# Seven experts' results turned by transposing DMAs of 16-bit planes and joined by VectorE, in place of TensorE's fp32 transposes

## What is computed

```python
for k in range(K):                       # K = 2 choices per token
    e = top_i[:, k]; w = top_p[:, k]
    ...                                  # place of the token in its expert's buffer, cap = 320
    buf = jnp.zeros((E, cap, D)).at[e, pos_c].set(xt * keep, mode='drop')
    h = gelu(jnp.einsum('ecd,edf->ecf', buf, w1) + b1[:, None, :])       # D = 512, f = 2048
    y = jnp.einsum('ecf,efd->ecd', h, w2) + b2[:, None, :]
    y = y + jnp.einsum('ecr,erd->ecd', gelu(jnp.einsum('ecd,edr->ecr', buf, wd)), wu)
    out = out + y[e, pos_c] * keep * w[:, None]
out = out + 0.2 * shared_expert(xt)
```

## Time and profile before

| | us |
|---|---|
| median of 3 executions | 1367.65 (1367.64 to 1367.82) |
| the profiled execution, its own time | 1367.89 |
| its span in the trace | 1366.1 |
| TensorE busy, share of the span | 96% |
| VectorE, ScalarE, GpSimd busy | 60%, 50%, 18% |
| mean granted clock of TensorE | 0.993 of full speed |

### The profile page before, as it was taken

One profiled execution on the slowest core, in us unless ns is written; L12 is line 12 of the kernel. 1 busy time (PEld: TensorE's weight loads), 2 busy tenths in 40 slices (PEclk: granted clock), 3 DMA queues, 4 the chain that ended last, 5 costly groups with the idle time before them and its releaser, 6 DMA issues.

```text
span 1366.1 us, 26996 instructions
## 1 busy us (share of the span) xinstructions
PE 1316.6 (96%) x11151; PEld 962.6 (70%) x11212; DVE 814.7 (60%) x1338; ACT 686.4 (50%) x1028; POOL 252.4 (18%) x219
## 2 busy tenths in 40 slices
PE   5788999999999999999999999999999999999997
PEld 2152736465564647384888889999999988888895
DVE  7786778697788887763643625536255363552620
ACT  4776666757576766662533524435244252442521
POOL 4730010000010050413200403003030040210202
PEclk9899999999999999999999999999999999999999
DMA  9613131413273232316635755457554675554403
GB/s 272 209 48 101 47 101 40 108 47 85 64 72 80 76 66 91 116 33 120 215 106 126 186 137 156 128 139 193 128 163 120 120 189 124 158 139 116 99 9 39
DMA packets 144939, 155.89 MB, mean 114 GB/s; under 512 B 67257, under 2 KB 87881, under 8 KB 144818
## 3 DMA queue, kind: packets, MB, share of 16 engines
q1 hardware_dynamic: 132530, 128.97, 34.8%
q0 software_dynamic: 12288, 25.21, 10.2%
HBM read 109.47 MB, written 34.15 MB: 105 GB/s over the span
## 4 chain that ended last, share of the span: by engine, by line
PE 82%; DVE 7%; ACT 6%; issue 4%; POOL 1%; DMA 0%; POOLq 0%; ACTq 0%; DVEq 0%
PE banks L1779 25%; PE banks L1809 24%; PE banks L1695 10%; PE banks L1713 9%; PE banks L1635 3%; PE banks L1583 3%; PE banks L1615 2%; DVE rowmax L1247 2%; ACT hidden L1036 2%; ACT QS L1023 2%; DVE late_stage L1268 1%; PE banks L1831 1%; PE banks L1644 1%; PE banks L1669 1%; ACT hf L1082 1%
## 5 line engine op out<-in xcount | busy, mean ns | idle before, releaser
L1809 PE MATMUL banks<-hidden,w2h 128*128 128x0 bf16 x2048 | 306.1, 269 | 0.0
L1036 ACT ACTIVATE hidden<-banks,scales 128x512 f32<-128x512 f32 x256 | 170.2, 686 | 102.8 <-PE banks L1615 66.9
L1809 PEld LDWEIGHTS banks<-hidden,w2h 128*128 128x128 bf16 x2048 | 198.6, 98 | 20.5
L1247 DVE TENSOR_REDUCE rowmax<-banks 128x1 f32<-128x512 f32 x256 | 172.4, 684 | 35.5 <-PE banks L1583 33.5
L1809 PE MATMUL banks<-hidden,w2l 128*128 128x0 bf16 x1024 | 192.3, 269 | 0.0
L1398 DVE TENSOR_TENSOR w1l<-stage,w1h 128x2048 bf16<-128x2048 f32 x32 | 73.2, 2291 | 191.3 <-ACT w1h L1113 191.3
L1130 ACT ACTIVATE hf<-banks,b1cols 128x640 f32<-128x640 f32 x128 | 101.4, 793 | 168.6 <-PE banks L1779 162.1
L1713 PE MATMUL banks<-w2h,hidden 128*128 128x512 bf16 x498 | 179.0, 379 | 1.8 <-issue 1.7
L1141 ACT ACTIVATE yT<-banks 128x640 f32<-128x640 f32 x28 | 19.7, 703 | 227.7 <-PE banks L1809 227.7
L1779 PE MATMUL banks<-eth,w1h 128*128 128x0 bf16 x1024 | 133.0, 273 | 0.0
L1779 PE MATMUL banks<-etl,w1h 128*128 128x0 bf16 x1024 | 132.9, 273 | 0.0
(11 more groups left out here) (195 smaller groups left out, 1970.4 us busy)
## 6 DMA issues: line engine op xcount, KB each, us to landing
stage<-in_L_ffn_w SPq DMA_DIRECT2D x64, 1024.0 KB
split_parts<-hidden SPq DMA_DIRECT2D x16, 512.0 KB, 5.6
QS<-split_parts SPq DMA_DIRECT2D x48, 128.0 KB, 2.7
KS<-split_parts SPq DMA_DIRECT2D x48, 128.0 KB, 3.1
xin<-in_x SPq DMA_DIRECT2D x16, 256.0 KB, 3.7
cin<-in_ctx SPq DMA_DIRECT2D x16, 256.0 KB, 3.3
out_rows<-xin SPq DMA_DIRECT2D x16, 256.0 KB, 2.0
normed_rows<-x2r SPq DMA_DIRECT2D x16, 256.0 KB, 3.4
```

The source lines that it names most:

```text
L1036: ac.activation(prob[n % NPH], bank(score_bank[unit]), ACT.Exp, scale=scales[:, g // 2:g // 2 + 1]).then_inc(s_exp, 1)
L1247: dv.reduce_max(rowmax[g % 2][:, i:i + 1], bank(score_bank[unit]), X_AXIS).then_inc(s_max, 1)
L1809: issued = mm(bank(b0 + j)[:, skips[j]:CAP].shape_from_register(used_cols(e, j)), w[:, fb, rows], of_choice(a[:, fb, :], j, skips[j]).shap ...
```

## The change

For the first seven experts the four fp32 transposes a chunk on TensorE are gone. In their place:

* ScalarE copies each down block from PSUM in two passes, one of the low and one of the high 16 bits of each word, into two planes that lie one behind the other in the memory of `yT`.
* SP issues two transposing DMAs for each d (`y_turn`), one for each plane, from 128 x 640 to 5 tiles of 128 x 128, into `turned_low` and `turned_high`. Those of d = 0, 1 and 2 stand in the list at (d, fb) = (1, 2), (2, 2) and (3, 12) of the down phase, that of d = 3 behind fb = 1 of the next expert's up phase.
* VectorE joins a chunk from the two planes into `yout` by two 16-bit copies of 128 x 512 that write every other 16-bit place. The chunks now stand behind fb = 5, 7, 9, 11 and 13.
* ScalarE multiplies `yout` by the slots' weights in place, after the join.

The last expert is as before.

```diff
+TURNS = [(1, 2), (2, 2), (3, 12)]
...
             add("e_up", e, fb)
             if fb == 1 and e + 1 < E:
                 add("gather", e + 1)
-            if e and fb % 2 and fb // 2 < CH:
-                add("e_y", e - 1, fb // 2)
+            if e and fb == 1:
+                add("y_turn", e - 1, KB - 1)
+            if e and fb % 2 and 0 <= fb - 5 < 2 * CH:
+                add("e_y", e - 1, (fb - 5) // 2)
...
                 add("e_down", e, d, fb)
+                if e + 1 < E and (d, fb) in TURNS:
+                    add("y_turn", e, TURNS.index((d, fb)))
...
+        turned_low = nc.alloc_sbuf_tensor_at("turned_low", [P, CH, D], U16, offset=xt_offset)
+        turned_rows = (turned_low, at("turned_high", [P, CH, D], U16, 2))
+
+        def y_part(d, a):
+            return yT[:, d, :].bitcast(U16)[:, a * SLOTS:(a + 1) * SLOTS]
...
+                elif kind == "y_turn":
+                    _, e, d = unit
+                    sp.wait_ge(s_ytc, KB * e + d + 1)
+                    if e and d == 0:
+                        sp.wait_ge(s_joined, CH * e)
+                    for a in range(2):
+                        dma(turned_rows[a][:, :, d * P:d * P + P], y_part(d, a), transpose=True).then_inc(s_yturn, 16)
...
+                    if e and d == 0:
+                        act.wait_ge(s_yturn, 16 * 2 * KB * e)
+                    if e < E - 1:
+                        for a in range(2):
+                            issued = ac.activation(by_choice(y_part(d, a)), halves(b0)[:, :, a::2], ACT.Copy)
+                        issued.then_inc(s_ytc, 1)
+                    elif skip:
...
                     n = e_y_no(e, c) - 1
-                    act.wait_ge(s_yt, e * CH + (c - first_block(e)) % CH + 1)
                     if e < E - 1:
-                        act.wait_ge(s_yst[n % 3], 16 * (n // 3))
-                    elif c == first_block(e):
+                        act.wait_ge(s_joined, e * CH + c + 1)
+                        if e == 0 and c == 0:
+                            act.wait_ge(s_table, 16)
+                        ac.activation(yout[n % 3][:, :], yout[n % 3][:, :], ACT.Copy,
+                                      scale=slots[:, e, c, 1:2].bitcast(F32)).then_inc(s_y, 1)
+                        continue
...
+        def halves(b):
+
+            return PB[:, b:b + 2, :].bitcast(U16)[:, :, 0:2 * CAP]
...
+                elif kind == "e_y" and unit[1] < E - 1:
+                    _, e, c = unit
+                    n = e_y_no(e, c) - 1
+                    dve.wait_ge(s_yturn, 16 * 2 * KB * (e + 1))
+                    dve.wait_ge(s_yst[n % 3], 16 * (n // 3))
+                    for a in range(2):
+                        issued = dv.tensor_copy(yout[n % 3][:, :].bitcast(U16)[:, a::2], turned_rows[a][:, c, :])
+                    issued.then_inc(s_joined, 1)
...
-                elif kind == "e_y" and unit[2] >= first_block(unit[1]):
+                elif kind == "e_y" and unit[1] == E - 1 and unit[2] >= first_block(E - 1):
```

More of the change, by code:

```diff
@@ L12 @@
 I32 = mybir.dt.int32
+U16 = mybir.dt.uint16
 ALU = mybir.AluOpType
@@ L513, in at @@
             return t
+        xt_offset = offset[0]
         xt_stage = nc.alloc_sbuf_tensor_at("xt_stage", [P, 2048], F32, offset=offset[0])
@@ L627, in build @@
         s_ytc, s_yt = sem("s_ytc"), sem("s_yt")
+        s_yturn, s_joined = sem("s_yturn"), sem("s_joined")
         CONSTANTS, FILLS = 9, NS + 3
@@ L1136, in act_program @@
                     skip = first_block(e) * P
-                    if skip:
+                    if e and d == 0:
[5 more added lines that the diff above has]
+                    elif skip:
                         ac.activation(yT[:, d, skip:CAP], bank(b0)[:, skip:CAP], ACT.Copy)
@@ L1144, in act_program @@
                     n = e_y_no(e, c) - 1
-                    act.wait_ge(s_yt, e * CH + (c - first_block(e)) % CH + 1)
                     if e < E - 1:
-                        act.wait_ge(s_yst[n % 3], 16 * (n // 3))
-                    elif c == first_block(e):
+                        act.wait_ge(s_joined, e * CH + c + 1)
[4 more added lines that the diff above has]
+                        continue
+                    act.wait_ge(s_yt, (c - first_block(e)) % CH + 1)
+                    if c == first_block(e):
                         act.wait_ge(s_wlo, 8 * E)
[L1150 to L1153, removed]
+                    ac.activation(last_rows[c][:, :], bank(4 + (e * CH + c) % 2 if c >= first_block(e) else 6), ACT.Copy,
                                   scale=slots[:, e, c, 1:2].bitcast(F32)).then_inc(s_y, 1)
@@ L1827, in pe_program @@
                     pe.wait_ge(s_ytc, KB * (e + 1))
-                    if m >= 2:
-                        pe.wait_ge(s_y, GROUPS + max(e * CH, m - 1 - first_block(e)))
+                    if c >= first_block(e) + 2:
+                        pe.wait_ge(s_y, GROUPS + m - 1 - first_block(e))
                     for d in range(KB):
```

## The result

The changed kernel takes 1398.10 us (median of 4 runs, 1393.19 to 1398.27); the kernel before, beside it on the same chip, 1367.74 (4 runs, 1367.64 to 1369.32). The ratio is 1.0203, 95% interval 1.0185 to 1.0220. Two later measurements of the same kernel gave 1.0167 [1.0151, 1.0184] and 1.0182 [1.0165, 1.0200]. So the change makes the kernel slower by 1.7 to 2.0%. The forecast was 1385 us, 1.3% slower.

A forecast was written before the change was run, and what follows sets the result against it. The prediction took TensorE's stream to bound the kernel, busy for 1316.6 us. From 1367.9, less 15.4 for transposes, plus 3.1 for the bank pair and 29.1 for the loop, it got 1384.7, predicting 1385 us, range 1371 to 1404.

The forecast's parts named there:

- TensorE's transposes, -15.4: TensorE's stream in the up phases: removing 35 chunks of four transposes, 0.44 us each, gives 15.4 us less.
- The other price in the prediction, 54.6 us for all 140: TensorE's 140 removed transposes at the Trainium skill's 390 ns each: an estimated 54.6 us, making the sum 1345.5.
- The bank pair, +3.1: After `e_rank`, TensorE waits 0.45 us for the bank pair under ScalarE's two copy passes, seven times: 3.1 us more.
- The serial loop, +29.1: Up phase: scaling, Gelu and join make ScalarE and VectorE take turns, so TensorE waits: 29.1 us more over seven experts.
- the rival of one element a cycle: VectorE's joins run one element a cycle, 1.29 us each: 15.1 us more, giving 1399.8; chance 0.17.
- the four-a-cycle estimate of 0.29: VectorE's join copy at the skill's four-a-cycle figure: an estimated 0.29 us, the sum about 1377.5.
- It waits 25.05 - 4P in all: TensorE's wait per expert from Gelu 7 to the down phase; P is two up blocks, 4.88 to 5.46 us.
- it would be there 8 blocks after Gelu 7: Without waiting, TensorE would reach the first down block 8 up blocks after Gelu 7 starts, at 4P (P: two blocks' time).
- the forecast (+16.9): Predicted lengthening from expert 1's first `e_rank` to TensorE's last matmul: sum of -15.4, 3.15 and 29.11 us.
- Transposes late: Transposing DMAs queue with 1 MB loads and come late for `e_rank` or joins: 1392 to 1399 us; chance 0.08.
- The hand-over hidden: Up phase: ScalarE and VectorE have room, so only removed transposes and bank pair count: 1355.6 us, faster; chance 0.12.

The follow-up runs named there:

- the kernel with both edits: Changed kernel with ScalarE's scaling one up block later and the bank-pair passes shared between ScalarE and VectorE: 1355.09 us against 1369.63, ratio 0.9896.
- the later scaling: Changed kernel with ScalarE's scaling of each chunk one up block later, the join staying in place: 1358.69 us, ratio 0.9921 to the kernel before.
- the stage without pauses (+22.0): Changed kernel without the gathers of experts 2 to 7: ratio 1.0172; expert 1's first `e_rank` matmul to TensorE's last is 22.0 us longer than before.

## Why the prediction was right in kind and low in size

* **TensorE's transposes, -15.4.** Right: 2.2 us an expert where nothing else is late, and all of it in the kernel with both edits. The other price in the prediction, 54.6 us for all 140, is out: with the transposes left out and nothing in their place the time fell by 13.4.
* **The bank pair, +3.1.** Measured 3.5 to 3.6. Two 16-bit passes over PSUM take 1.30 us, for which 1.31 was worked out; 16-bit reads of every other place are as fast as the fp32 copy (701 against 703 ns). The rest is the 0.06 of overlap between `e_rank` and the first up block, which the wait ends: the pair costs 0.51 an expert, not 0.45.
* **The serial loop, +29.1.** The mechanism and its place are shown by the later scaling. The loops were 8.11, 4.79 and 8.11 against 8.03, 4.71 and 8.03; the scaling held ScalarE for 0.63 instead of 0.57 (1137.36 to 1137.99), which is most of the 0.08. The join took 0.79 (1136.54 to 1137.33) for 0.75, so the rival of one element a cycle (1.29) is out. The Trainium skill, "Vector Engine (DVE) Microarchitecture Reference", section 5.1, has two results a cycle for such a copy whatever its step; the copies' 0.45 us, near the 0.416 of the fp32 cast of as many elements, agree, and the four-a-cycle estimate of 0.29 does not hold at step two.
* **Where the size failed.** The step is the third one's sum, "It waits 25.05 - 4P in all". Measured from the start of Gelu 7 to the down phase it is 25.38 in experts 4 to 6 of the changed kernel: the last scaling comes at 23.93 instead of 23.65, and TensorE 1.46 after it instead of 1.40. In expert 7 it is 25.78, as its first down block starts 0.45 after the even Gelu's end, elsewhere 0.06; in the last expert TensorE's program sets the width of these matmuls from a register just ahead of them, which may be the 0.4, but no run tests that. And "it would be there 8 blocks after Gelu 7" was a little generous: Gelu 7 starts 0.2 behind the slot of the next block (0.16 of overlap and 0.04 of hand-over), so TensorE waits 0.2 longer. For seven experts that makes 7 x 0.33 + 0.40 + 7 x 0.2 = 4.1, and with 0.4 for the bank pair 4.5 of the 5.1 us by which the stage without pauses (+22.0) exceeded the forecast (+16.9). Most of the remaining 0.6 is expert 2, whose first join comes 0.5 later.
* **What was not in the sum at all** are ScalarE's pauses: up to 3.4 us. In the kernel before, the longest, of 1.2 us, cost nothing. The loop is not needed for them to count: with the later scaling a pause of 2.9 in expert 1 still made TensorE wait 1.1 us.
* **Together**: 16.9 + 5.1 + 3.4 = 25.4 of the 25.5 in the profiled execution, which at 1393.19 lies 25.3 over that of before. The 5.1 and 3.4 are differences between stages, so that this sum comes out by itself; worked out apart from it are 4.5 of the 5.1, and the pauses expert by expert. The other three executions of that measurement took 1398.04 to 1398.27. They were not traced, and what their 5 us are stays open. The part ahead of the experts, which varied by 3.5 us between traces of this kernel, is one candidate, but that is only argued. The two later measurements gave 1.0167 and 1.0182, so the forecast of 1.013 was low by 0.4 to 0.7% of the time.
* **Transposes late**: not so. TensorE's waits ahead of `e_rank` for DMAs are not in the trace, and leaving the transposes out changes nothing. A transpose of five tiles held SP for 1.28 us (median of 56, 1.20 to 2.34), where 1.6 was assumed; one of four tiles takes as long (median 1.27).
* **The hand-over hidden** was a rival of 0.12. It was wrong for this order and right for one place further: its 1355.6 is a ratio of 0.9910, and the kernel with the later scaling came to 0.9921 [0.9906, 0.9935].

## What to carry to other kernels

An operation split into a part on one in-order engine and a part on another puts everything queued behind it into a loop with both. Sums of busy time say nothing of that: VectorE had 11 us free per up phase before the change and the loop still set the time. Walk the chain once round (who waits for the second part, and what does the first engine's next work wait for), and put the consumer at least one step of the pipeline behind its producer. Here moving one table entry by one up block turned 1.7% slower into 0.8% faster.

## What the runs showed of the hardware

* A wait of TensorE behind a group of 128 x 128 matmuls cost its stream 0.16 us more than the idle time shown beside it, as the groups of a running stream overlap by that much in the trace (1.87 against 0.89 from start to start, with 0.82 shown). Behind the short matmuls of `e_rank` it was 0.06.
* A 16-bit copy of 128 x 512 from SBUF on VectorE that writes every other place took 0.45 us, 0.34 from start to start when two follow each other. ScalarE's 128 x 640 read of every other 16-bit place of PSUM took 0.70 us, as its fp32 read does.
* ScalarE paused 0.3 to 2.9 us ahead of a Gelu, with nothing in the trace that it waited for, at the place where five gathers were issued and, around the longest pause, the DMA share was 1.08; without gathers there it did not. What it waits for in that time is not known.
